# Loads, index tiles and small vector pieces of a table-building stage put at other places

## The chip, the cores and the metric

The kernel runs on one core of a Trainium2 chip. The metric is the device time of one execution in microseconds (us). The engines of the core run side by side and meet only at semaphores: TensorE (PE, with its weight loads shown as PEld), VectorE (DVE), ScalarE (ACT), GpSimd (POOL) and SyncE (SP, which issues transfers here and computes nothing). POOL issues transfers too. All transfers share 16 DMA engines.

## What is computed

One transformer layer in float32: latent cross-attention and then a gated feed-forward, each behind a layer norm and with a residual sum. The first stage, which the change touches, turns 16 context sequences of 361 rows into one table of latent and rotated keys, and folds the per-head weights.

```python
kv_c = kv @ W_kvc                       # 16 sequences, 361 rows, 512 -> 128
q_c = q @ W_dq                          # q = layernorm(x), 16 x 100 rows
k_nope = (kv_c @ W_uk); v = (kv_c @ W_uv); k_rope = _rope(kv_c @ W_kr, lk)
scores = (q_nope . k_nope + q_rope . k_rope) * scale
good = (k_ids <= qs) & (k_ids >= qs - LOOKBACK)      # qs = seg_id
scores = jnp.where(good[:, None, :, :], scores, NEG)
x = x + softmax(scores) @ v @ W_o
x = x + ffn(layernorm(x))
```

Each query looks at 9 keys only. They are gathered from the table by an index that is worked out from seg_id.

## The kernel before

Three stages follow each other: the table stage (build_setup, a block of its own that all engines enter and leave together), the attention over 5 blocks of 320 tokens, and the feed-forward over the same blocks. The change lies in the table stage.

**Turns.** The table stage has 16 turns, one for each context sequence n and, at the same time, for each head n. In each turn:
- SP loads the context `ctx_raw` (4 buffers) and the head's weights `head_w` (2 buffers). The first ones are issued ahead. From then on `head_w` n waits until turn n-2's weights have been read (`v_mm`, `r_lo`, the latter counted by DVE's last split of a turn), and `ctx_raw` n+2 follows it in the queue.
- ACT writes the high part of the context with its sums and means (`ctx_hi`, L345 to L352; 2 buffers). After that it takes the previous turn's results out of PSUM (`tab_part` L359, `wl_hi` L362, `wvo_hi` L365, `wr_hi` L368).
- DVE writes the low part (`ctx_lo`, L455) and then the previous turn's `tab` (L431) and weight remainders (L438 to L450). `tab` has 2 buffers, so L431 waits until the table store of two turns earlier has landed.
- PE multiplies the context with the folded weights: 9 high products (L487), then low and high ones (L497, L487), then the head's products with `head_w` (L509, L512). The low ones wait for `ctx_lo`. L509 waits for the load of `head_w`.
- POOL rotates the key part of `tab` (L308 to L315) and stores it into `kv_table` (L317).

Turns 0 to 3 are written out; 4 to 15 are a loop of three passes of four (`turns`).

**Small work beside the turns.** DVE's `index_work` (L404 to L419) makes the gather index `idx_all` and two mask tiles. It stands at the end of DVE's turn 0. Its seven tiles lie in the place of the second `ctx_hi` buffer, so ACT may touch that buffer only after `index_ok` (L373, at the head of its turn 1). DVE's norm pieces for the first token block (`ln.piece`: 0 to 3 statistics of a fourth of the rows, 4 the variance, 5 and 6 the normalising) stand in turns 0 (pieces 0 to 3), 1, 2 and 3. Piece 0 waits for the load of `rows` (x). POOL takes the root after its turn 0. DVE's `key_mask_work` (five operations, L395 to L399) stands behind the last turn. At the end PE turns the normalised rows (L569) and multiplies them with `wdq` (L168).

**Loads.** SP issues them in the order of its text: weights, context 0, index and mask constants, context 1, head 0, x, context 2, head 1, context 3. POOL issues five constants (`ident`, `mask`, `cosq`, `sinq`, `wdq`) before its first turn.

## Time and profile before

| | |
|---|---|
| median of 3 runs | 806.59 us (807.15, 806.59, 794.01) |
| profiled execution | 795.53 us, its span 793.9 us |
| PE busy in the span | 736.8 us (93%) |
| DVE, ACT, POOL busy | 452.4, 407.3, 196.5 us |
| table stage | 0 to 111.95 us |
| DMA over the span | 102 GB/s on average |
| loads of the table stage besides contexts and heads | weights 256 + 32 + 256 KB; index and mask 494 KB (six); x 640 KB; POOL's five constants 64 + 31.5 + 240 + 480 + 512 KB; POOL's other first ones 48 + 96 + 6 KB |

The span is the time from the first to the last instruction of the profiled execution; the device time is 1.6 us more. Where a row gives a wait, it stands in square brackets with what ended it. "x9" is a group of nine instructions that the view has merged. The three runs lie 13 us apart, and the profiled execution is near the lowest of them.

### The profile page before, as it was taken

How to read it: one execution, taken by the hardware profiler on the slowest of the kernel's cores; microseconds unless marked ns; L12 is line 12 of the kernel's file. 1: busy time of each engine (PE TensorE's matmuls, PEld its weight loads, DVE VectorE, ACT ScalarE, POOL GpSimd, SP SyncE). 2: the span in 40 equal slices, each digit the busy share in tenths (PEclk: the TensorE clock that was granted, in tenths of full speed). 3: DMA queues.
4: the chain of work that ended last, by engine and by line, in shares of the span. 5: the costliest groups of instructions: out<-in, count | busy, mean ns of one | idle time of the engine just before them, and what ended most of it. 6: DMA issues, size and time to landing. Idle time of an engine off the chain costs nothing.

```text
span 793.9 us, 18186 instructions
## 1 busy us (share of the span) xinstructions
PE 736.8 (93%) x7102; PEld 689.5 (87%) x7102; DVE 452.4 (57%) x944; ACT 407.3 (51%) x899; POOL 196.5 (25%) x330
## 2 busy tenths in 40 slices
PE   3799987789999899989999999989999999999997
PEld 3688777578997799879997899779999999999997
DVE  2887863463467555665477446755693363636342
ACT  3688834275456644575457645666577232313131
POOL 2455552542217140534044131530000000000000
PEclk9999998798999999999999999999999999999999
DMA  8899844444330533134322343047101102121021
GB/s 263 250 307 306 281 137 107 90 112 79 72 97 4 128 85 89 37 110 89 73 68 89 63 86 104 3 162 310 50 18 34 50 20 67 33 66 33 22 62 34
DMA packets 46357, 81.19 MB, mean 102 GB/s; under 512 B 5482, under 2 KB 30106, under 8 KB 46282
## 3 DMA queue, kind: packets, MB, share of 16 engines
q1 hardware_dynamic: 40796, 53.67, 26.2%
q0 software_dynamic: 5488, 26.50, 9.9%
q8 instruction: 52, 0.85, 0.5%
q14 instruction: 21, 0.17, 0.1%
HBM read 57.26 MB, written 11.28 MB: 86 GB/s over the span
## 4 chain that ended last, share of the span: by engine, by line
PE 70%; DVE 5%; ACT 4%; SPq 2%; DMA 2%; issue 1%; POOL 0%; another core or an unknown queue 0%; DVEq 0%; POOLq 0%
PE ps L1350 18%; PE ps L1059 12%; PE ps L927 9%; PE ps L1382 9%; PE ps L1064 6%; PE ps L1002 3%; PE ps L168 3%; PE ps L975 3%; SPq L827 2%; ACT q_lat L1102 2%; PE ps L937 2%; DMA key_rows<-kv_table,idx 1%; PE ps L966 1%; PE ps L991 1%; PE ps L772 1%
## 5 line engine op out<-in xcount | busy, mean ns | idle before, releaser
L1206 DVE TENSOR_TENSOR o_lo<-q_lat,o_hi 128x320 fp32r<-128x320 f32 x80 | 70.5, 887 | 81.1 <-ACT o_hi L1110 77.9
L1059 PE MATMUL ps<-o_hi,wvo_hi 128*128 128x320 f32 x320 | 96.8, 313 | 1.8 <-ACT o_hi L1110 1.8
L1110 ACT ACTIVATE o_hi<-q_lat 128x320 fp32r<-128x320 f32 x80 | 65.5, 825 | 62.2 <-PE ps L1059 61.1
L1059 PE MATMUL ps<-o_hi,wvo_lo 128*128 128x320 f32 x320 | 95.7, 310 | 0.0
L1434 ACT ACTIVATE silu<-ps,ffn_scale 128x320 f32<-128x320 f32 x55 | 29.0, 527 | 97.5 <-PE ps L1350 97.5
L869 POOL TENSOR_TENSOR rot_c<-gathered,cosq 128x192 f32<-128x192 f32 x40 | 25.4, 635 | 173.8 <-PE ps L937 143.4
L1485 DVE SCALAR_TENSOR_TENSOR hidden<-ps,ffn_scale,silu 128x320 f32<-128x320 f32 x55 | 30.2, 549 | 60.5 <-ACT silu L1434 52.8
L1059 PEld LDWEIGHTS ps<-o_hi,wvo_hi 128*128 128x128 f32 x320 | 60.6, 189 | 2.3 <-ACT o_hi L1110 2.0
L1059 PEld LDWEIGHTS ps<-o_hi,wvo_lo 128*128 128x128 f32 x320 | 60.5, 189 | 0.3
L1064 PE MATMUL ps<-o_lo,wvo_hi 128*128 128x320 f32 x320 | 60.2, 309 | 0.0
L487 PE MATMUL ps<-wkv,ctx_hi 128*128 128x384 f32 x192 | 52.9, 385 | 6.5 <-ACT ctx_hi L352 6.5
L557 POOL TENSOR_TENSOR lnf_rstd<-lnf_var,lnf_power 80x4 f32<-80x4 f32 x5 | 5.1, 1017 | 197.0 <-DVE lnf_var L551 197.0
L1350 PE MATMUL ps<-rowsT,hi_front 128*128 128x320 f32 x280 | 53.5, 308 | 0.0
L1350 PE MATMUL ps<-four,hi_front 128*128 128x320 f32 x280 | 53.1, 311 | 0.0
L1064 PEld LDWEIGHTS ps<-o_lo,wvo_hi 128*128 128x128 f32 x320 | 50.6, 189 | 0.0
L487 PEld LDWEIGHTS ps<-wkv,ctx_hi 128*128 128x128 f32 x192 | 36.4, 198 | 14.0 <-issue 13.4
L1120 ACT ACTIVATE q_lat<-ps 128x320 f32<-128x320 f32 x40 | 31.9, 798 | 32.1 <-PE ps L927 32.1
L1002 PE MATMUL ps<-probT,gathered 63*128 63x112 f32 x480 | 37.7, 290 | 11.2 <-ACT probT L1094 9.6
L1002 PEld LDWEIGHTS ps<-probT,gathered 63*128 63x128 f32 x480 | 30.6, 190 | 17.3 <-ACT probT L1094 11.8
L1350 PEld LDWEIGHTS ps<-rowsT,hi_front 128*128 128x128 f32 x280 | 44.2, 188 | 0.0
L1350 PEld LDWEIGHTS ps<-four,hi_front 128*128 128x128 f32 x280 | 43.6, 188 | 0.0
L878 POOL TENSOR_TENSOR rot<-rot_c,rot_s 128x384 f32<-128x384 f32 x40 | 42.7, 1067 | 3.1
(170 smaller groups left out, 1884.9 us busy)
## 6 DMA issues: line engine op xcount, KB each, us to landing
ctx_raw<-ctxT_dram SPq DMA_DIRECT2D x16, 722.0 KB, 7.6
gathered<-key_rows SPq DMA_DIRECT2D x240, 47.2 KB
head_w<-head_w_dram SPq DMA_DIRECT2D x16, 576.0 KB, 5.3
ffn_raw<-ffn_w_dram POOLq DMA_DIRECT2D x11, 768.0 KB, 12.8
kv_table<-tab POOLq DMA_DIRECT2D x16, 288.0 KB, 6.6
rows<-x_dram SPq DMA_DIRECT2D x5, 640.0 KB, 5.3
residual<-x_dram SPq DMA_DIRECT2D x20, 160.0 KB, 2.4
x_rows<-residual SPq DMA_DIRECT2D x20, 160.0 KB, 2.0
```

The costliest lines, as they stand in the source:

```text
L487: return pe.matmul(ps[:, b + t, 0:2 * ROW], hi[i % 2][:, c, t * P:(t + 1) * P], wkv[:, c, :], start=(c == 0), stop=(c == KC - 1), skip_gro ...
L878: pool.tensor_tensor(rot[s % 2][:, :, :, :], rc[:, :, :].unsqueeze(2).to_broadcast([GR, GROUPS, 2, R]), rs[:, :, :].unsqueeze(2).to_broadc ...
L927: last = pe.matmul(ps[:, q_bank(o), 0:TB], w[wt][:, hs, :].rearrange("p h c -> p (h c)"), xs[:, :], start=(n == 0), stop=(n == len(parts) ...
L1002: last = pe.matmul(ps[:, 6 + side, g * SK:(g + 1) * SK], kvg[keys, s, g, 0:KVC], pt[s % 2][keys, g * SK:(g + 1) * SK], start=True, stop=True)
L1059: last = pe.matmul(ps[:, 4 + m, 0:TB], w[wt][:, h, cols], o_hi[h % 2][:, :], start=(h == 0 and n == 0), stop=False, skip_group_check=True)
L1064: last = pe.matmul(ps[:, 4 + m, 0:TB], w["wvo_hi"][:, h, m * P:(m + 1) * P], o_lo[h % 2][:, :], start=False, stop=(h == H - 1), skip_group ...
L1110: act.activation(o_hi[h % 2][:, :], q_lat[:, h % 2, :, h // 2], ACT.Copy).then_inc(oh_ok, 1)
L1120: act.activation(q_dst(o), ps[:, q_bank(o), 0:TB], ACT.Copy).then_inc(q_act, 1)
L1206: dve.tensor_tensor(o_lo[h % 2][:, :], q_lat[:, h % 2, :, h // 2], o_hi[h % 2][:, :].bitcast(F32), ALU.subtract).then_inc(ol_ok, 1)
L1350: return pe.matmul(ps[:, 2 * which + c % 2, 0:TB], wt(part, c, which, k), xs[:, k, :], skip_group_check=True, **flags)
L1382: return pe.matmul(ps[:, 4 + m % 2, 0:TB], wt(part, c, 2, m), xs[:, c, :], skip_group_check=True, **flags)
L1485: dve.scalar_tensor_tensor(out=hf[:, c % 2, :], in0=ps[:, 2 + c % 2, 0:TB], scalar=scale[:, IC + c:IC + c + 1], in1=act_g[:, c % 2, :], op ...
```

## The change

It touches build_setup alone. The seven index tiles get a place of their own behind the other tiles, and ACT clears both `ctx_hi` buffers ahead of turn 0 and waits for `index_ok` no more. SP's first loads stand in another order, with x last. POOL's five constants move from ahead of turn 0 to behind its turn 2. `index_work` moves from DVE's turn 0 to its turn 1. The norm pieces 0 to 6 move to turns 4 to 10, one in each, with the root behind POOL's turn 7. The five operations of the key mask move to turns 11 to 15, one in each. DVE's and POOL's 16 turns are written out, where 12 of them were a loop.

```diff
-        with ExitStack() as index:
-            segw = sb("segw", [WROWS, BLOCKS * WSETS], I32, index)
...
+        segw = sb("segw", [WROWS, BLOCKS * WSETS], I32)
...
                 load_ctx(0, 0)
-                for dst, name in ((segw, "segw"), (segm, "segm"), (base, "row_base"), (edge_of, "edge_of")):
+                load_head(0, 0)
+                load_ctx(1, 1)
+                load_ctx(2, 2)
+                load_head(1, 1)
+                for dst, name in ((segw, "segw"), (base, "row_base"), (segm, "segm"), (edge_of, "edge_of")):
                     sp.dma_start(dst[:, :], a[name]).then_inc(seg_in, 16)
                 sp.dma_start(other32[:, :], a["other"]).then_inc(mask_in, 16)
                 sp.dma_start(blocks32[:, :], a["blocks"]).then_inc(mask_in, 16)
-                load_ctx(1, 1)
-                load_head(0, 0)
+                load_ctx(3, 3)
                 sp.dma_start(rows[:, :, :], a["x"][0:TB, :].rearrange("(t p) d -> p t d", p=LT)).then_inc(x_in, 16)
-                load_ctx(2, 2)
-                load_head(1, 1)
-                load_ctx(3, 3)
...
-                    if isinstance(n, int) and n == 0:
+                    if isinstance(n, int) and n == 2:
+                        pool.dma_start(ident[:, :], a["ident"]).then_inc(const_in, 16)
...
+                        pool.dma_start(w["wdq"][:, :, :], a["wdq"]).then_inc(const_in, 16)
+
+                for n in range(NB):
+                    rope(n, n // 4, n % 4)
+                    if n == 7:
                         ln.root(pool, 0)
-
-                turns(pool, rope)
...
-                for half in (*lo, hi[0]):
+                for half in (*lo, *hi):
...
-                    if isinstance(n, int) and n == 1:
-                        act.wait_ge(index_ok, 1)
-                        act.activation(hi[1][:, :, LK + MEANS:TROWS], zero[:, :, :], ACT.Copy)
...
-                    if isinstance(n, int) and n == 0:
+                    if n == 1:
                         index_work()
-                    if isinstance(n, int):
-                        for piece in ((0, 1, 2, 3), (4,), (5,), (6,))[n]:
-                            ln.piece(dve, 0, piece, x_in)
-
-                turns(dve, turn)
+                    elif 4 <= n < NLT + 7:
+                        ln.piece(dve, 0, n - 4, x_in)
+                    elif NLT + 7 <= n:
+                        key_mask_piece(n - NLT - 7)
+
+                for n in range(NB):
+                    turn(n, n // 4, n % 4)
                 low_weights(NB - 1, 0, NB - 1)
-                key_mask_work()
```

`key_mask_piece(k)` is operation k of `key_mask_work`, unchanged.

On SP's queue the loads ahead of the loop read as follows before the change, in the order of issue (`four` is where the folded weights' parts land, `rows` is x):

```order
L252 DMA ctx_raw<-ctxT_dram 128x4x361
L264 DMA segw<-segw_dram 126x15
L264 DMA segm<-segm_dram 128x640
L264 DMA row_base<-row_base_dram 126x15
L264 DMA edge_of<-edge_of_dram 128x2
L265 DMA other<-other_dram 128x128
L266 DMA blocks<-blocks_dram 128x189
L252 DMA ctx_raw<-ctxT_dram 128x4x361
L256 DMA head_w<-head_w_dram 128x1152
L269 DMA rows<-x_dram 80x4x512
L252 DMA ctx_raw<-ctxT_dram 128x4x361
L256 DMA head_w<-head_w_dram 128x1152
```

After the change the same queue, from the first context on:

```order
L253 DMA ctx_raw<-ctxT_dram 128x4x361
L257 DMA head_w<-head_w_dram 128x1152
L253 DMA ctx_raw<-ctxT_dram 128x4x361 x2
L257 DMA head_w<-head_w_dram 128x1152
L269 DMA segw<-segw_dram 126x15
L269 DMA row_base<-row_base_dram 126x15
L269 DMA segm<-segm_dram 128x640
L269 DMA edge_of<-edge_of_dram 128x2
L270 DMA other<-other_dram 128x128
L271 DMA blocks<-blocks_dram 128x189
L253 DMA ctx_raw<-ctxT_dram 128x4x361
L273 DMA rows<-x_dram 80x4x512
```

Head 0 and contexts 1 and 2 and head 1 have passed the index and mask constants, and x has gone behind context 3.

On DVE, from its turn 0 to the head of its turn 1, before the change (`ctx_lo` opens a turn; `lnq_st` are the norm's statistics, which wait for x):

```order
L455 TENSOR_TENSOR ctx_lo<-ctx_raw,ctx_hi 128x4x370
L405 CAST segf<-segw 126x15
L406 TENSOR_SCALAR empty<-segf 126x15
...
L416 CAST other<-other 128x128
L417 CAST blocks<-blocks 128x189
L419 MEMSET done_mark 1x1
L543 BN_STATS lnq_st<-rows 80x6 x4
L455 TENSOR_TENSOR ctx_lo<-ctx_raw,ctx_hi 128x4x370
L431 TENSOR_TENSOR tab<-ps,tab_part 128x576
```

The same engine after the change, from turn 0 to turn 2:

```order
L460 TENSOR_TENSOR ctx_lo<-ctx_raw,ctx_hi 128x4x370 x2
L436 TENSOR_TENSOR tab<-ps,tab_part 128x576
L443 TENSOR_TENSOR wl_lo<-ps,wl_hi 128x128
...
L455 TENSOR_TENSOR wr<-head_w,wr 64x64
L410 CAST segf<-segw 126x15
...
L422 CAST blocks<-blocks 128x189
L424 MEMSET done_mark 1x1
L460 TENSOR_TENSOR ctx_lo<-ctx_raw,ctx_hi 128x4x370
```

Nothing stands between the first two `ctx_lo` any more. The index operations stand behind turn 0's remainders, and the statistics are gone from here.

## Rows read from the trace of the kernel before

**Rows 1.** Chain of work that ended last, stretch 0 to 150: start, us, what.
```profile
111.95 0.02 POOLq L248
...
113.04 11.75 DMA key_rows<-kv_table,idx
```
**Rows 2.** Windows: busy us (count) of PE, PEld, DVE, ACT, POOL; clock; DMA.
```profile
9.00:26.60 17.60, 8.20 (x39) 7.01 (x39) 8.52 (x20) 9.08 (x36) 0.00 (x0) 1.00 1.04 322
26.60:30.40 3.80, 3.78 (x17) 3.78 (x18) 3.58 (x13) 0.37 (x3) 2.57 (x6) 0.55 0.18 32
35.00:96.00 61.00, 57.50 (x351) 49.99 (x350) 51.27 (x85) 50.85 (x188) 32.69 (x69) 1.00 0.96 308
14.00:16.00 2.00, 2.00 (x7) 2.00 (x8) 1.90 (x5) 0.00 (x0) 0.00 (x0) 1.00 1.07 376
```
**Rows 3.** Timeline of turns 0 and 1: start us, us, engine, line, operation, [wait].
```profile
7.84 0.84 ACT L337 ACTIVATE wkv<-four 128x768 fp32r<-128x768 f32 x1
11.12 0.51 ACT L345 ACTIVATE ctx_hi<-ctx_raw 128x361 fp32r<-128x361 f32 x1 [2.44 <-DMA ctx_raw<-ctxT_dram]
17.91 0.25 ACT L374 ACTIVATE ctx_hi<-zero 128x56 fp32r<-128x56 f32 x1 [4.20 <-DVE done_mark L419]
22.50 2.47 DVE L543 BATCH_NORM_STATS2 lnq_st<-rows 80x6 f32<-80x512 f32 x4 [4.62 <-DMA rows<-x_dram]
29.11 0.35 SPq L256 DMA_DIRECT2D head_w<-head_w_dram  x1
```
**Rows 4.** Timeline, PE: the head's products of turns 0, 2, 14 and 15.
```profile
19.31 0.71 PE L509 MATMUL ps<-head_w 128*128 128x128 f32 x4 [0.49 <-DMA head_w<-head_w_dram]
34.96 0.60 PE L509 MATMUL ps<-head_w 128*128 128x128 f32 x4
98.20 0.68 PE L509 MATMUL ps<-head_w 128*128 128x128 f32 x4 [0.72 <-DMA head_w<-head_w_dram]
103.03 0.61 PE L509 MATMUL ps<-head_w 128*128 128x128 f32 x4
```
**Rows 5.** Transfers: out, in, queue, count, KB each, median us to landing.
```profile
ctx_raw<-ctxT_dram SPq DMA_DIRECT2D x16, 722.0 KB, 7.6
head_w<-head_w_dram SPq DMA_DIRECT2D x16, 576.0 KB, 5.3
kv_table<-tab POOLq DMA_DIRECT2D x16, 288.0 KB, 6.6
wdq<-wdq_dram POOLq DMA_DIRECT2D x1, 512.0 KB, 9.0
```
**Rows 6.** Waits in 35 to 96: who, on whom: us, times, longest.
```profile
DVE tab L431 <- DMA kv_table<-tab: 4.4, 8, 1.1
DVE ctx_lo L455 <- ACT ctx_hi L352: 4.0, 7, 0.9
PE ps L509 <- DMA head_w<-head_w_dram: 3.4, 5, 1.3
```
**Rows 7.** Timeline, DVE: two `ctx_lo` without a wait between, and two pieces.
```profile
39.37 1.17 DVE L561 TENSOR_SCALAR rows<-rows,lnq_mv,lnq_rstd 80x512 f32<-80x512 f32 x2
40.46 1.69 DVE L455 TENSOR_TENSOR ctx_lo<-ctx_raw,ctx_hi 128x1480 fp32r<-128x1480 f32 x1
44.71 1.98 DVE L455 TENSOR_TENSOR ctx_lo<-ctx_raw,ctx_hi 128x1480 fp32r<-128x1480 f32 x1
```
**Rows 8.** Timeline, end of the stage: PE's product with wdq, DVE's key mask.
```profile
106.55 0.77 DVE L395 CAST key_wanted<-segm 128x640 f32<-128x640 int32 x1
107.21 4.57 PE L168 MATMUL ps<-rowsT,wdq 128*128 128x320 f32 x16 [0.53 <-ACT rowsT L578]
109.62 0.55 DVE L399 TENSOR_SCALAR edge<-key_inside,edge_of 128x640 bf16<-128x640 f32 x1
```
**Rows 9.** Timeline: one turn's tab on DVE and its store on POOL.
```profile
63.27 0.76 DVE L431 TENSOR_TENSOR tab<-ps,tab_part 128x576 f32<-128x576 f32 x1 [0.51 <-DMA kv_table<-tab]
67.23 0.80 POOL L317 DMA_DIRECT2D kv_table<-tab  x1 [0.88 <-POOL tab L315]
```

More of the change, by code:

```diff
@@ L224, in build_setup @@
         hw = [sb(f"head_w{i}", [P, HW]) for i in range(2)]
+        segw = sb("segw", [WROWS, BLOCKS * WSETS], I32)
+        base = sb("row_base", [WROWS, BLOCKS * WSETS], F32)
+        segf = sb("segf", [WROWS, BLOCKS * WSETS], F32)
+        empty = sb("empty", [WROWS, BLOCKS * WSETS], F32)
+        over = sb("over", [WROWS, BLOCKS * WSETS], F32)
+        other32 = sb("other32", [P, P], F32)
+        blocks32 = sb("blocks32", [P, GROUPS * GK], F32)
         w_in, kr_in, seg_in, rk_in, const_in, mask_in = (
@@ L237, in build_setup @@
         chain, x_in, front_in = sem("index_chain"), sem("first_rows_in"), sem("front_rows")
+        edge_ok = sem("edge_ok")
         index_ok, done_mark = sem("index_ok"), sb("done_mark", [1, 1])
@@ L294, in _ @@
                 pool.dma_start(sink[:, :, :], a["sink"]).then_inc(rk_in, 16)
-                pool.dma_start(ident[:, :], a["ident"]).then_inc(const_in, 16)
-                pool.dma_start(w["mask"][:, :], a["mask"]).then_inc(const_in, 16)
-                pool.dma_start(w["cosq"][:, :, :], a["cosq"]).then_inc(const_in, 16)
-                pool.dma_start(w["sinq"][:, :, :], a["sinq"]).then_inc(const_in, 16)
-                pool.dma_start(w["wdq"][:, :, :], a["wdq"]).then_inc(const_in, 16)
                 pool.wait_ge(rk_in, 32)
@@ L391, in link, with key_mask_piece @@
                     dve.wait_ge(chain, done[0])
-                def key_mask_work():
-                    link(dve.tensor_copy(wanted[:, :], segm[:, :]))
-                    link(dve.tensor_scalar(wanted[:, :], wanted[:, :], edge_of[:, 0:1], None, ALU.add))
-                    link(dve.tensor_scalar(inside[:, :], wanted[:, :], 0.0, float(LK - 1), ALU.max, ALU.min))
-                    link(dve.tensor_tensor(inside[:, :], inside[:, :], wanted[:, :], ALU.not_equal))
-                    link(dve.tensor_scalar(w["edge"][:, :, :].rearrange("p s x -> p (s x)"), inside[:, :],
-                                           edge_of[:, 1:2], None, ALU.mult))
+                def key_mask_piece(k):
+                    if k == 0:
+                        link(dve.tensor_copy(wanted[:, :], segm[:, :]))
+                    elif k == 1:
+                        link(dve.tensor_scalar(wanted[:, :], wanted[:, :], edge_of[:, 0:1], None, ALU.add))
+                    elif k == 2:
+                        link(dve.tensor_scalar(inside[:, :], wanted[:, :], 0.0, float(LK - 1), ALU.max, ALU.min))
+                    elif k == 3:
+                        link(dve.tensor_tensor(inside[:, :], inside[:, :], wanted[:, :], ALU.not_equal))
+                    else:
+                        dve.tensor_scalar(w["edge"][:, :, :].rearrange("p s x -> p (s x)"), inside[:, :],
+                                          edge_of[:, 1:2], None, ALU.mult).then_inc(edge_ok, 1)
                 def index_work():
```

9 lines of the change are left out of this document (3 added, 6 removed).

## The prediction

> **What bounds the kernel now.** PE is busy for 93% of the span, so I did not ask the whole span what bounds it, but the stage that is changed; nothing behind it is touched. The chain of work gives the stage's end: all engines leave the block at 111.95, and 1 us later the first gather starts, whose 11.75 us are on the chain [rows 1]. Whatever the stage loses or gains is therefore passed on in full, and the 682 us behind it are taken as unchanged.
>
> Inside the stage I asked which resource sets the pace of a turn. A turn moves 722 + 576 + 288 = 1586 KB, or 1.624 MB [rows 5]. From 35 to 96 the DMA engines have a share of 0.96 and move 308 GB/s [rows 2]. 1.624 MB at that rate are 5.27 us. PE's products with `head_w` start at 34.96 in turn 2 and at 98.20 in turn 14, so a turn takes 63.24 / 12 = 5.27 us [rows 4]. The two agree. PE alone would be quicker: from turn 14 to 15, where it waits for nothing, it takes 4.83 us [rows 4]. In that stretch it waits 3.4 us for `head_w` itself [rows 6], and it also comes later because ACT and DVE do. So from turn 2 on the stage is bound by transfers, with PE 0.44 us a turn behind.
>
> The start is different. ACT could begin context 0 when the folded weights are ready, at 7.84 + 0.84 = 8.68, but it waits for the load until 11.12. It then waits 4.20 us for DVE's index work, because of the shared place. DVE waits 4.62 us for x and only then makes turn 1's `ctx_lo`; PE waits for that in turn [rows 3]. As turn 0's remainders on DVE stand behind all this, SP can issue `head_w` 2 only at 29.11 [rows 3]. Its queue has run dry by then: from 26.6 to 30.4 the DMA engines have a share of 0.18 and move 32 GB/s [rows 2]. PE's granted clock is 0.55 of full speed in that stretch, after PE has waited.
>
> **The change part by part.**
>
> *The start.* The index tiles' own place takes ACT's 4.20 us away. The moved pieces take DVE's 4.62 us away. The loads' order takes 11.12 - 8.68 = 2.4 us off context 0, since 1327 KB of POOL's constants no longer run beside it. PE's product with `head_w` of turn 0 comes at 19.31 - 0.49 - 2.4 = 16.4. Two turns at PE's own pace later, at 16.4 + 2 x 4.83 = 26.1, comes that of turn 2, where it was at 34.96 [rows 4]. That is a lead of 8.9 us. The loads allow it: up to head 1 they are 256 + 32 + 256 + 2166 + 1152 KB and POOL's 150 KB, 4.1 MB, which at 322 GB/s [rows 2] have come some 13 us after the first start of a transfer at about 3.
>
> *What the lead is worth.* The bytes that must have come before PE's product of turn 14 are the same before and after: every context, heads 0 to 14, x, the index and mask constants and POOL's five (1327 KB, of which `wdq` is 512 [rows 5]; the others are in the table above). Only their order changes. The 1.36 MB of POOL's constants and x's 0.66 MB now fall behind turn 2, and cost (1.36 + 0.66) / 0.308 = 6.6 us there. So where transfers bound, the end moves by the DMA's idle time that is taken out, and by nothing else: 3.8 us x (1 - 32 / 308) = 3.4 us [rows 2]. The remaining 5.5 us of the lead turn into waits for `head_w` at PE. I see no new gap: x is the last of the first loads, at (4.1 + 0.5 + 0.74 + 0.66) MB / 322 GB/s + 3 = 22 us, and `head_w` 2 may be issued when turn 0's remainders are done. These ended just before 29.11, when `head_w` 2 was issued; they now start when ACT has turn 0's results, some 3 us behind 16.4, and end at about 20.
>
> *The pieces in turns 4 to 15.* DVE's turn without a wait is 44.71 - 40.46 = 4.25 us [rows 7]. The pieces are four statistics (2.47 us in all [rows 3]), the variance (0.6, an estimate: as long as one statistic), two normalisings of about 1.1 [rows 7], and the key mask, 109.62 + 0.55 - 106.55 = 3.62 [rows 8]. Together 8.9 us, or 0.74 a turn: 4.99 against the transfers' 5.27. Only the turns with a normalising, 5.35, are above it, by 0.1 us each. What covers the pieces is DVE's waiting, 4.4 + 4.0 us in the twelve turns [rows 6], most of which ends because a transfer has come. Were that cover gone, each piece would be paid. A late DVE issues `head_w` late, but there is always a context in the queue ahead of it: one lands 7.6 us after its issue, and the next head's issue comes 5 us after it [rows 5]. I take 0, with 0 and 2 us as bounds.
>
> *The index work in turn 1.* Its 2.5 us (it held ACT until 17.91 and began behind turn 0's `ctx_lo`, near 15.4) stand between turn 0's remainders (about 20) and `ctx_lo` of turn 2, needed at 24. It waits for the mask constants, which are due at about (4.1 + 0.5) / 0.322 + 3 = 17. I take 0; the bound is 1 us.
>
> *POOL.* Five issues make its rotation of turn 3 late once, by at most 5 x 0.80 = 4.0 us if each costs what the table store's issue does [rows 9], and by nothing if POOL would have waited for DVE anyway. Table stores have 2 buffers, so this reaches DVE at turn 5 and is hidden as long as transfers bound. Written out, a turn has no register work before its store; I count nothing for it.
>
> *The key mask's old place.* DVE ended there at 110.17, while PE ended at 107.21 + 4.57 = 111.78 [rows 8]. Taking it away gains nothing. PE's tail from turn 15's product to the end, 111.78 - 103.03 = 8.75 us, stays.
>
> The sum is -3.4 us against the profiled execution: 795.5 - 3.4 = 792.1, with a span of 790.5. Two of the three runs of before are near 807 and one is 13 us below, beside the profiled one, a spread four times my sum. The median of the runs is 806.6, and against it the sum gives 803.2. I state that one, since the median is the time that is compared, but the range must hold both levels.
>
> **A rule that would make more of it.** The Trainium skill, DMA: Bandwidth & Descriptors, in its Specifications, gives an HBM limit of about 358 GB/s for a core. By it a turn's 1.624 MB would be an estimated 4.54 us, under PE's 4.83, PE would set the pace, and the lead would be kept. The row for the turns does not agree with it: 308 GB/s at a share of 0.96.
>
> **The rivals.**
>
> *The lead is kept (0.18).* The engines have moved 376 GB/s where loads ran alone [rows 2]; a turn would need 1.624 / 4.83 = 336. If the 308 are no limit of the engines but what a stage in lockstep with PE, ACT and DVE asks for, PE sets the pace. Its product of turn 15 comes at 26.1 + 13 x 4.83 = 88.9 in place of 103.03: -14.1 us, 781.4 (792.5 at the median's level). Against it speaks that PE waits for `head_w` at all, and the share of 0.96.
>
> *The gap comes back elsewhere (0.12).* The two queues together run less well when POOL's constants meet the steady stream, or the index work is late. Then the end stays: 0 us, 795.5 (806.6).
>
> *The table store's loop closes (0.08), the slower side.* `tab` has 2 buffers. From DVE's `tab` to the store's issue are 67.23 - 63.27 = 3.96 us [rows 9], then 6.6 us to the landing [rows 5]: 10.6 us for two turns, the present pace. If each piece stood between a landing and the next `tab`, two of them (1.48) and a landing of 7.4 would make 12.84 us, 6.42 a turn. Then turn 15's product comes at 26.1 + 4.83 + 12 x 6.42 = 108.0, +5.0 us: 800.5 (811.6). It decides from (103.03 - 30.9) / 12 = 6.01 us a turn. For it speaks that DVE waits for this very store 8 times [rows 6]. Against it, the pieces stand ahead of `ctx_lo`, where DVE waits too. SBUF — State Buffer, section Who interferes with whom, of the Trainium skill says that a fast VectorE copy or tensor_scalar locks GpSimd out of a shared port; that would make the store later still. No row of before shows such a piece beside a store.
>
> **How the numbers follow.** The forecast (-3.4) has 0.62. Its own range is -6 to -1 us, that is 789.5 to 794.5 or 800.6 to 805.6 by the level. A measurement of this kernel can tell about 2% from no change, which is 16 us. None of the cases reaches that like for like; the largest is 14.1 us. If the levels of the two kernels should fall apart, 13 us come on top, and so I give faster 0.08, same 0.90, slower 0.02. The range takes in the forecast at both levels and no change at the upper one, 807, and half of the kept lead below the lower one, 786.
>
> **What would show it.** In the profile after: no stretch under 200 GB/s between 10 and 95 us; turn 1's `ctx_lo` near 15 and turn 2's product with `head_w` near 26; `head_w` 2 issued near 20; PE's waits for `head_w` up from 3.4 to about 8 us; turns of about 5.3 us; turn 15's product near 99.6 and the block left near 108.5. DVE's waits shrink by about the pieces' 8.9 us. The prediction is wrong if turns take 4.9 us or less (the first rival), if DVE's waits for the store grow (the third), or if something behind the stage changes its length by more than 1 us.

## The result and the profile after

| | before | after |
|---|---|---|
| median of 20 runs each, us | 796.03 (791.20 to 807.15) | 792.01 (787.27 to 805.49) |
| profiled execution, us | 795.53 | 787.27 |
| its span, us | 793.9 | 785.5 |
| its PE busy | 93% | 730.4 us, 93% |
| PE's product with `head_w` of turn 15 starts at | 103.03 [rows 4] | 97.86 |
| all engines leave the block at | 111.95 [rows 1] | 106.78 |
| from there to the end of the span | 681.95 | 678.72 |

The ratio of the times is 0.9945, with a 95% interval from 0.9927 to 0.9963: the change gains 0.55%, or 4.4 us, which is no change by the 2% that was named. The forecast of -3.4 us was nearly the size of it. The stated 803.2 is 11 us above the median of after, inside the range, and it is above before's 796.03 too. Two of before's 20 runs and five of after's lie 11 to 12 us above the others, the three runs of before that the prediction had to go by held two of these, and the ratio compares the runs without them.

The profiled execution of after is the quickest of its 20, so its own 8.3 us under the one of before (8.4 by the spans) are not the size of the change. 5.17 of the 8.4 are the stage. The other 3.23 us lie behind the stage, where no instruction was changed; 2.3 of these are one group, sixteen products of PE in the first attention block, PE's timeline of before and then of after:

```profile
182.71 6.85 PE L168 MATMUL ps<-rowsT,wdq 128*128 128x320 f32 x16
```

```profile
178.35 4.55 PE L168 MATMUL ps<-rowsT,wdq 128*128 128x320 f32 x16
```

A second profiled execution of the changed kernel (changed_again, below) took 791.96 us, 4.7 more than the first. 2.7 of these lie behind the stage as well, so the 3.23 us are little more than two executions of one program differ by.

The rows of after that answer to [rows 4], the head's products; columns as there. Shown are turns 0, 2, 5, 6, 14 and 15:

```profile
16.78 0.60 PE L515 MATMUL ps<-head_w 128*128 128x128 f32 x4
...
26.64 0.68 PE L515 MATMUL ps<-head_w 128*128 128x128 f32 x4
...
45.95 1.20 PE L515 MATMUL ps<-head_w 128*128 128x128 f32 x4 [3.21 <-DMA head_w<-head_w_dram]
52.34 0.60 PE L515 MATMUL ps<-head_w 128*128 128x128 f32 x4
...
93.05 0.68 PE L515 MATMUL ps<-head_w 128*128 128x128 f32 x4
97.86 0.61 PE L515 MATMUL ps<-head_w 128*128 128x128 f32 x4
```

Turn 2 comes at 26.64, 8.3 us ahead of before's 34.96. Between turns 2 and 6 a turn takes (52.34 - 26.64) / 4 = 6.43 us, and at turn 6 the lead is down to 3.1 us (before's turn 6 comes at 55.40). From turn 6 to 15 a turn takes (97.86 - 52.34) / 9 = 5.06, where before takes (103.03 - 55.40) / 9 = 5.29, and the lead grows again to 5.17.

Windows of after, columns as in [rows 2]. From 54 to 96 DVE, the third pair of numbers, is busy for 40.75 of 42 us:

```profile
0.00:9.00 9.00, 1.97 (x8) 1.78 (x8) 0.96 (x1) 3.45 (x9) 2.17 (x8) 1.00 0.68 209
9.00:26.00 17.00, 14.12 (x80) 12.87 (x81) 11.16 (x25) 13.26 (x51) 3.53 (x8) 1.00 1.04 321
26.00:30.00 4.00, 4.00 (x25) 3.42 (x24) 3.92 (x6) 3.14 (x13) 2.34 (x6) 1.00 0.62 193
30.00:36.00 6.00, 6.00 (x42) 5.52 (x42) 5.17 (x9) 3.91 (x15) 5.54 (x12) 1.00 0.94 299
36.00:50.00 14.00, 9.41 (x46) 7.44 (x46) 9.82 (x17) 8.37 (x33) 7.07 (x16) 0.88 1.03 388
50.00:54.00 4.00, 4.00 (x28) 3.52 (x27) 3.30 (x6) 3.33 (x14) 1.41 (x2) 1.00 0.51 137
54.00:96.00 42.00, 40.24 (x248) 35.38 (x248) 40.75 (x73) 35.60 (x131) 24.63 (x49) 1.00 0.93 302
0.00:98.00 98.00, 81.73 (x484) 71.94 (x485) 76.95 (x138) 71.07 (x259) 48.35 (x103) 0.98 0.89 293
```

And of before, for the stretches that the prediction did not look at:

```profile
0.00:9.00 9.00, 1.97 (x8) 1.78 (x8) 0.28 (x1) 3.31 (x8) 4.80 (x13) 1.00 0.67 182
9.00:26.00 17.00, 8.20 (x39) 7.01 (x39) 7.92 (x19) 8.51 (x34) 0.00 (x0) 1.00 1.05 325
26.00:34.00 8.00, 7.38 (x38) 6.90 (x39) 7.65 (x21) 4.13 (x17) 6.00 (x12) 0.79 0.50 148
30.00:32.00 2.00, 2.00 (x10) 1.52 (x10) 2.00 (x3) 1.28 (x4) 1.98 (x2) 0.92 0.92 251
32.00:34.00 2.00, 2.00 (x16) 2.00 (x15) 1.87 (x6) 2.00 (x10) 1.86 (x6) 1.00 0.79 238
0.00:103.00 103.00, 82.33 (x482) 72.26 (x483) 73.42 (x133) 71.18 (x259) 48.71 (x104) 0.98 0.88 279
```

The last row of each is the argument of the prediction in two lines. Up to turn 15's product the kernel of before moves 103 us x 279 GB/s = 28.7 MB, the changed one 98 x 293 = 28.7 MB. The bytes are the same, and what the stage gained is a higher mean rate. Where it comes from, each stretch held against the 308 GB/s of [rows 2]: before loses (308 - 148) x 8 us = 1.28 MB, or 4.2 us, in one stretch from 26 to 34. After loses (308 - 193) x 4 + (308 - 299) x 6 + (308 - 137) x 4 = 1.20 MB in three stretches, and makes up (388 - 308) x 14 = 1.12 MB between 36 and 50, which leaves 0.25 us. The first 9 us give (209 - 182) x 9 = 0.24 MB, or 0.8 us. 4.2 - 0.25 + 0.8 = 4.7 of the 5.2 us; the rest is spread over rows that differ by a few GB/s.

Of this account only the sum holds for the program. In the second execution of the changed kernel the mean up to 98 us is 293 GB/s again and turn 15 comes at 98.18, but the first 9 us have 184 GB/s, and the stretch from 50 to 54, a hole above, has none:

```profile
50.00:54.00 4.00, 4.00 (x27) 3.48 (x26) 3.47 (x6) 3.52 (x14) 2.17 (x5) 1.00 1.03 359
```

So the 0.8 us of the first 9 us are no gain of the change, and where the low stretches lie differs from one execution to the next.

SyncE's queue in after shows what stands ahead of the two low stretches at 26 and at 50; start, us, engine, line, operation:

```profile
20.85 0.58 SPq L253 DMA_DIRECT2D ctx_raw<-ctxT_dram  x1
27.28 0.34 SPq L257 DMA_DIRECT2D head_w<-head_w_dram  x1
...
43.05 0.56 SPq L253 DMA_DIRECT2D ctx_raw<-ctxT_dram  x1
51.19 0.34 SPq L257 DMA_DIRECT2D head_w<-head_w_dram  x1
```

It issues nothing for 6.4 and for 8.1 us. The issue at 27.28 waits for turn 1's remainders on DVE, which stand behind the index work. The one at 51.19 waits for turn 5's, and turn 5's product had waited 3.21 us for its `head_w`, issued at 37.25 when POOL's constants, the issues below, were in flight:

```profile
33.18 0.58 POOL L316 DMA_DIRECT2D ident<-ident_dram  x1
...
35.35 0.53 POOL L320 DMA_DIRECT2D wdq<-wdq_dram  x1
```

The waits of after between 30 and 92 us, columns as in [rows 6]:

```profile
PE ps L515 <- DMA head_w<-head_w_dram: 6.3, 4, 3.2
...
ACT ctx_hi L348 <- DMA ctx_raw<-ctxT_dram: 4.6, 2, 3.1
DVE ctx_lo L460 <- ACT ctx_hi L355: 3.9, 3, 3.0
...
DVE tab L436 <- DMA kv_table<-tab: 0.7, 1, 0.7
```

PE's waits for `head_w` are 6.3 us (4.8 in the second execution) where [rows 6] has 3.4, and DVE's waits for the table store are nearly gone, 0.7 for 4.4.

### The profile page after: what moved, and what is told of

It reads as the page before. It is cut to its first block, busy times and chain, and to the rows that moved or that the text cites. A ratio compares the mean times of both kernels' runs of the same rounds, so it can differ in the third digit from the quotient of the medians.

```text
span 785.5 us, 18041 instructions
## 1 busy us (share of the span) xinstructions
PE 730.4 (93%) x7102; PEld 684.7 (87%) x7102; DVE 455.2 (58%) x944; ACT 407.9 (52%) x899; POOL 197.0 (25%) x330
## 3 DMA queue, kind: packets, MB, share of 16 engines
q1 hardware_dynamic: 40796, 53.67, 26.1%
## 4 chain that ended last, share of the span: by engine, by line
PE 71%; ACT 4%; DVE 4%; DMA 2%; SPq 2%; issue 1%; POOL 0%; DVEq 0%; POOLq 0%
PE ps L1356 18%; PE ps L1065 12%; PE ps L933 9%; PE ps L1388 9%; PE ps L1070 6%; PE ps L1008 3%; PE ps L981 3%; PE ps L168 2%; SPq L833 2%; ACT q_lat L1108 2%; PE ps L943 2%; DMA key_rows<-kv_table,idx 2%; PE ps L972 2%; PE ps L997 1%; PE ps L778 1%
## 5 line engine op out<-in xcount | busy, mean ns | idle before, releaser
L1100 ACT ACTIVATE probT<-ps 63x336 f32<-63x336 f32 x80 | 35.3, 442 | 15.6 <-PE ps L997 11.3
```

Of the source, the lines that this page charges most:

```text
L1100: act.activation(pt[s % 2][side * HALF:side * HALF + GK, :], ps[0:GK, 4 + side, 0:GROUPS * SK], ACT.Copy).then_inc(p_ev, 1)
```

## Experiments

Two theories were held against each other from the start. By theory 1 transfers set the pace, the end moves only by the DMA's idle time that goes, and the lead is given back. By theory 2 the engines' own work and lockstep (DVE with its pieces, POOL's loop, the table store) set the pace, and what gains is moving or removing their work. Where an expectation says for its run what each theory means, that holds. "Turn 15" stands for the start of PE's head product of turn 15, "left" for the time at which all engines leave the block.

| kernel | turn 0 | turn 15 | left | us (runs) | ratio to before |
|---|---|---|---|---|---|
| before | 19.31 | 103.03 | 111.95 | | |
| pool_written_out | 19.52 | 103.08 | 112.00 | 794.62 (10) | 0.9982 [0.9955, 1.0009] |
| norm_moved | 18.74 | 98.60 | 107.52 | 791.56 (6) | 0.9939 [0.9897, 0.9982] |
| own_place | 18.77 | 102.02 | 110.95 | 793.55 (1) | |
| after | 16.78 | 97.86 | 106.78 | 792.01 (20) | 0.9945 [0.9927, 0.9963] |
| changed_again | 18.88 | 98.18 | 108.78 | 790.20 (7) | 0.9927 [0.9897, 0.9957] |
| heads_cut | 17.08 | 93.30 | 102.30 | 787.80 (1) | |
| dve_more | 17.26 | 100.69 | 109.68 | 793.35 (1) | |
| mask_last | 17.08 | 98.49 | 107.41 | 789.15 (1) | |
| consts_late | 17.40 | 95.45 | 105.64 | 791.11 (10) | 0.9940 [0.9907, 0.9973] |
| consts_first | 18.30 | 99.49 | 108.41 | 788.77 (4) | 0.9904 [0.9882, 0.9926] |
| index_last | 17.78 | 97.68 | 108.29 | 789.01 (5) | 0.9905 [0.9873, 0.9937] |
| sp_order_old | 17.42 | 97.16 | 107.77 | 801.77 (1) | |
| best | 17.21 | 95.66 | 106.27 | 789.59 (9) | 0.9924 [0.9891, 0.9957] |

The intervals of the changed kernels overlap, but for those of consts_first and after, which miss each other by 0.0001, and changed_again's overlaps both; the times rank none of them. What tells them apart is the trace of the stage, where the same kernel comes to turn 15 within 0.3 us (97.86 and 98.18). That is one pair of executions, and each other kernel has one trace, so a difference of less than about 0.5 us at turn 15 is not read as an effect. At turn 0 the same pair is 2.1 us apart (16.78 and 18.88), and no difference of that size is read as one there. The pair also shows the lead being given back: 2.1 us at turn 0 have become 0.3 at turn 15.

**pool_written_out**: the kernel before with one edit, POOL's loop written out.

```diff
-                turns(pool, rope)
+                for n in range(NB):
+                    rope(n, n // 4, n % 4)
```

> The kernel before, with POOL's 16 turns written out and nothing else changed. Theory 1 (transfers alone set the pace of a turn, 1.624 MB at 308 GB/s): the 0.4 us that POOL saves ahead of each table store are worth nothing; turn 2 to turn 14 of PE's head product stay 63.2 us apart, the stage ends at 111.9, the time is that of before within 0.5 us. Theory 2 (the table store's loop over its two buffers bounds together with the transfers): the pace falls from 5.27 towards 5.05 us a turn, DVE's waits for the store fall from 4.4 us to about 1, and the stage ends about 2 us earlier.

Measured: turn 15 at 103.08 for 103.03, and no difference in time that the interval shows. The waits between 30 and 95 us, of this kernel and then of before:

```profile
DVE ctx_lo L456 <- ACT ctx_hi L353: 7.4, 10, 1.3
```

```profile
DVE ctx_lo L455 <- ACT ctx_hi L352: 4.0, 7, 0.9
```

DVE's waits for the table store fall from 4.4 to 2.1 us, and its waits for ACT's `ctx_hi` grow from 4.0 to 7.4. The wait only changed its name. A wait that shrinks while the turns keep their length was no bound, and POOL's loop was none.

**norm_moved**: the kernel before, with only the norm's pieces moved to turns 4 to 10 (POOL's and DVE's loops written out for it, which the last run showed to be worth nothing on POOL; DVE's was not tried alone).

```diff
-                    if isinstance(n, int):
-                        for piece in ((0, 1, 2, 3), (4,), (5,), (6,))[n]:
-                            ln.piece(dve, 0, piece, x_in)
+                    if 4 <= n < NLT + 7:
+                        ln.piece(dve, 0, n - 4, x_in)
```

> The kernel before with one part of the change: the norm pieces go to turns 4 to 10, with the root behind POOL's turn 7, and DVE's and POOL's turns are written out. Loads, index work and its place as before. DVE no longer waits for x in turn 0, ACT still waits for the index work. Theory (the hole in the transfers at 26.6 to 30.4 was what DVE's wait for x cost): turn 1's ctx_lo comes at 20.7 in place of 24.9, head load 2 is issued at 25 in place of 29.1, the hole closes, and the stage ends 3 to 4 us earlier, near 108.5. If the loads' order is what matters, as x and the constants stand ahead of context 2: at most 1 us.

Measured: turn 15 comes at 98.60, 4.4 of the change's 5.2 us. Turn 1's `ctx_lo` starts at 19.98 and `head_w` 2 is issued here:

```profile
24.23 0.35 SPq L256 DMA_DIRECT2D head_w<-head_w_dram  x1
```

That is 4.9 us before the 29.11 of [rows 3]. The window where before had its hole [rows 2]:

```profile
26.60:30.40 3.80, 3.80 (x29) 3.66 (x28) 3.68 (x8) 3.74 (x16) 1.71 (x5) 1.00 0.96 348
```

348 GB/s for 32. So the norm's pieces in turns 0 to 3 are the cause of nearly all of it, and not by the time that DVE stood still: by holding the remainders of turn 0, they held SyncE's next issue, and the queue ran dry. Most of that is the wait of 4.62 us for x; the 2.47 us of statistics behind it moved with it, and no run takes the two apart. Against this kernel the whole change is only 0.4 to 0.7 us earlier at turn 15.

**own_place**: the kernel before, with only the index tiles in a place of their own and ACT's wait gone.

```diff
-                for half in (*lo, hi[0]):
+                for half in (*lo, *hi):
...
-                    if isinstance(n, int) and n == 1:
-                        act.wait_ge(index_ok, 1)
-                        act.activation(hi[1][:, :, LK + MEANS:TROWS], zero[:, :, :], ACT.Copy)
```

> The kernel before with one part of the change: the index tiles get their own place and ACT's wait for the index work goes. ACT then makes turn 1's ctx_hi up to 4 us earlier, but DVE is busy with the index work until 17.9 and waits for x until 22.5, so ctx_lo comes at 24.9 as before. Expected: 0 us, the stage ends at 112 plus or minus 0.5, head load 2 at 29.1. If ACT's wait was part of the path: up to 4 us earlier.

Measured: turn 15 at 102.02, 1.0 us earlier, of which turn 0 has 0.5. Turn 1's `ctx_lo` starts at 24.01 (24.88 in before), still behind a wait of 4.12 us for x, and `head_w` 2 is issued at 28.23. The first context was taken up 0.4 us earlier here too (10.75 for 11.12), where nothing was changed, so the 1.0 us is an upper bound. ACT's 4.20 us of [rows 3] lay beside DVE's wait for x: with one of two parallel waits gone, the other holds.

**heads_cut**: the changed kernel, but from head 2 on only the first 128 of `head_w`'s columns are loaded (its folded head weights are therefore not the model's). A turn moves less, and PE, ACT and DVE do the same work.

```diff
+                    cols = HW if isinstance(n, int) and n < 2 else P
+                    sp.dma_start(hw[i][:, 0:cols], a["head_w"][bass.ds(n, 1), :, 0:cols]
```

> The changed kernel, but from head 2 on only the first 128 of 1152 columns of the head's weights are loaded, so the folded head weights are wrong; all instructions and waits stay. That takes 512 of 1586 KB out of each turn. If transfers bound the turns: PE's waits for the head load vanish and the turns go to PE's own 4.75 to 4.83 us throughout, turn 15's head product comes near 91 in place of 97.9. If DVE with its pieces bounds now (4.25 plus 0.74 a turn): turns stay near 5.0 and turn 15's product comes near 94 or later, with DVE idle for under 0.1 us a turn.

Measured: turn 15 at 93.30, 4.6 us earlier than after. All of it is gained at the stall: from turn 2 to 6 the kernel takes 4.82 + 4.74 + 6.11 + 4.84 = 20.51 us, where after takes 25.70 and changed_again 23.25. The 6.11 is turn 5 again: its load, now of 64 KB, is issued at 36.52 and waited for until 42.62, with POOL's constants in flight beside it. From turn 6 to 15 the kernel takes 45.84, where after takes 45.52. Its turns 6 to 9 have 4.75 to 4.86 us, PE's own pace, but then turns of 5.06 to 5.47 come. DVE's timeline tells why; one turn of it, with the pieces ahead of each `ctx_lo`:

```profile
78.26 0.77 DVE L399 TENSOR_SCALAR key_wanted<-key_wanted,edge_of 128x640 f32<-128x640 f32 x1
79.06 1.70 DVE L461 TENSOR_TENSOR ctx_lo<-ctx_raw,ctx_hi 128x1480 fp32r<-128x1480 f32 x1
...
83.33 0.77 DVE L401 TENSOR_SCALAR key_inside<-key_wanted 128x640 f32<-128x640 f32 x1
84.14 1.70 DVE L461 TENSOR_TENSOR ctx_lo<-ctx_raw,ctx_hi 128x1480 fp32r<-128x1480 f32 x1
```

No row of DVE between the two `ctx_lo`, 5.08 us apart, carries a wait. So transfers bound the changed kernel up to the stall's end, and each theory is right for a part: behind it, with much of the head's bytes gone, DVE and its pieces hold the stage at the same pace that after has with all of them. The changed kernel's own rows say the same: from 54 to 96 DVE waits once, for 0.6 us, and in changed_again never, where before's DVE is busy for only 33.80 of these 42 us. That bound lies only 0.2 us a turn below the transfers' 5.27.

**dve_more**: the changed kernel with a further statistic on a tile at rest in each of turns 4 to 15, which adds DVE work and no transfer.

```diff
+                    if 4 <= n:
+                        dve.bn_stats(scratch[:, n, :], idle_in[:, :])
```

> The changed kernel with one more statistic of 512 columns on DVE in each of turns 4 to 15, of 0.62 us and 7.4 us in all; its result goes to a scratch tile that nobody reads. DVE's turn is then 4.25 + 0.74 + 0.62 = 5.6 us on average. If DVE still has cover (transfers at 5.06 to 5.27 us a turn, waits of 4.6 us left): turn 15's product comes about 12 x (5.6 - 5.27) = 4 us later, near 101 to 102, since its own pace now passes that of the transfers. If pieces cost nothing as long as any wait is left: 98 to 99. If they are paid in full: 105.

Measured: turn 15 at 100.69, 2.8 us later, for 12 x 2.47 / 4 = 7.4 us of work ([rows 3] has the length of four statistics). A wait stands in its list (30 to 92 us) that after's does not have:

```profile
PE ps L509 <- DVE ctx_lo L464: 1.9, 4, 0.8
```

So 2.8 of the 7.4 us arrive at turn 15. That is not because waits cover the rest: behind the stall there are hardly any left, and the turns grow at once. From one `ctx_lo` to the next DVE takes 0.43 to 0.61 us more than in after in turns 7 to 10, and 0.19 to 0.38 more in turns 11 to 14. The first three statistics fall ahead of the stall's end, where DVE waits anyway: at turn 6 the kernel is only 0.2 us behind after. And the key mask's pieces become shorter. The second of them, in after and then in dve_more:

```profile
82.44 0.77 DVE L398 TENSOR_SCALAR key_wanted<-key_wanted,edge_of 128x640 f32<-128x640 f32 x1
```

```profile
85.25 0.53 DVE L400 TENSOR_SCALAR key_wanted<-key_wanted,edge_of 128x640 f32<-128x640 f32 x1
```

In after it lies beside POOL's last operation on `tab`:

```profile
82.22 0.64 POOL L311 TENSOR_TENSOR tab<-rope_cos,rope_sin 128x192 f32<-128x192 f32 x1
```

In dve_more the statistic stands in front of it, and POOL is done. Four of these pieces lie ahead of turn 15's product; together they take 3.44 us in after and 2.27 in dve_more. The expected 101 to 102 was nearest, though not for the reason given, cover by transfers. That POOL's work is what lengthens the pieces is argued from the rows, no run was made for it.

**mask_last**: the changed kernel with the five key mask pieces behind the last turn, where they stood before.

```diff
-                    elif NLT + 7 <= n:
-                        key_mask_piece(n - NLT - 7)
...
+                for k in range(5):
+                    key_mask_piece(k)
```

> The changed kernel with one part undone: the five operations of the key mask stand behind DVE's last turn again. If the pieces in turns 11 to 15 are covered by transfers: turns 11 to 15 keep their pace of about 5.05 us. If DVE bounds there (with the heads cut it ran at 5.07 a turn in just these turns): they go to 4.9 us and turn 15's product comes up to 1 us earlier, near 97. DVE ends near 105 and PE's last product near 106.6, so the old place costs nothing at the end.

Measured: turn 15 at 98.49, left at 107.41, against 97.86 and 106.78 of after. DVE's waits for `ctx_hi` (30 to 95 us) are 7.1 us instead of 3.9: without the pieces DVE waits, and the turns 11 to 15 are no shorter (5.12 us on average, 5.04 in after). So DVE alone does not set their pace either; the transfers' bound of 5.27 lies right beside it, but what binds in these turns no row shows for sure. The mask pieces gained nothing and cost nothing.

**consts_late**: the changed kernel with POOL's constants later still: `ident` and `wdq` behind turn 11, mask, cosq and sinq behind turn 14.

```diff
-                    if isinstance(n, int) and n == 2:
+                    if n == 11:
...
+                    if n == 14:
+                        pool.dma_start(w["mask"][:, :], a["mask"]).then_inc(late_in, 16)
```

> The changed kernel with POOL's constants still later: ident and wdq behind turn 11, mask, cosq and sinq behind turn 14, where the engines' transfers have nearly run out; PE waits for the first two. If transfers bound up to the last head, the 752 KB that leave the bound stretch are worth 0.77 MB / 0.308 = 2.5 us, the stall of 3.2 us at turn 6 disappears, and a smaller one comes at turn 13: the stage ends 2 to 3 us before 106.7 (profile), the time is 0.3% below the changed kernel. If they were hidden anyway (their burst ran at 392 GB/s): no difference within 0.5 us.

Measured: turn 15 at 95.45, 2.4 us earlier than after. The stall at turn 5 is gone (turn 4 to 5 is one of 4.8 us) and between 36 and 50 PE is busy for 12.95 us, where it was for 9.41:

```profile
36.00:50.00 14.00, 12.95 (x80) 11.06 (x79) 12.76 (x21) 11.84 (x45) 7.68 (x16) 1.00 0.99 325
```

(The expectation counts this turn as the sixth.) It shows that it was POOL's constants that held back turn 5's `head_w`. Of the 2.4 us only 1.1 reach the end (left at 105.64): PE's last product is done at 104.20, and the block is left 1.4 us later. It is not the constants that are waited for, since SyncE's wait for `sinq` is over 2.7 us before the block is left; what remains is POOL's wait for the last table store, issued at 101.46 behind the three constants. That is argued, no run shows it. In the time nothing of it can be seen.

**consts_first**: the changed kernel with the five constants ahead of POOL's turn 0 again, as in before.

> The changed kernel with one part undone: POOL's five constants are loaded ahead of turn 0 again. Turn 0 comes 2.4 us later. Theory of bytes (the end is set by the sum of the bytes and the holes): the stall of 3.2 us at turn 6 goes, turn 15's head product stays at 97.9 plus or minus 1. If the order itself is worth something, the start's 2.4 us are lost to the end: 100.3.

Measured: turn 0 comes at 18.30 and turn 15 at 99.49, 1.3 to 1.6 us later than in the two executions of the changed kernel; the time is not worse (0.9904). The slow start is not the reason: changed_again's turn 0 is later still, and at turn 6, with no stall behind it, this kernel is ahead of both (50.97 for 52.34 and 51.98). It falls back from turn 6 to 15, at 5.39 us a turn for 5.06 and 5.13, with 4.4 us of waits for `head_w` at PE from 52 to 98 us where changed_again has 2.2. In the two others the transfers had run ahead during the stall. Why they fall behind here was not settled.

**index_last**: the changed kernel with the index work behind the last turn's low weights.

```diff
-                    if n == 1:
-                        index_work()
-                    elif 4 <= n < NLT + 7:
+                    if 4 <= n < NLT + 7:
...
+                index_work()
```

> The changed kernel with the index work behind DVE's last turn, where DVE has nothing to do while PE finishes. Head load 3 is then issued about 2.6 us earlier (27.3 to 24.7), and the hole in the transfers at 26 to 29 us (119 to 156 GB/s) closes. If transfers bound behind it, the stage ends 1 to 1.5 us earlier (the bytes that the hole did not carry). If the later stall is set by the constants alone, or the lockstep takes the lead back: 0 to 0.5 us. At the end DVE's work of 2.6 us ends before PE's last product either way.

Measured: the stretch 24 to 32 of this kernel, and then of after:

```profile
24.00:32.00 8.00, 8.00 (x54) 7.52 (x54) 6.96 (x14) 7.39 (x28) 4.85 (x11) 1.00 0.91 288
```

```profile
24.00:32.00 8.00, 7.92 (x54) 7.02 (x53) 7.75 (x15) 6.97 (x27) 4.86 (x11) 1.00 0.77 246
```

(288 - 246) x 8 us are 0.34 MB, 1.1 us at 308 GB/s; turn 15 comes at 97.68, 0.2 to 0.5 us earlier. But the hole is not closed, it lies earlier: from 20 to 24 the windows have 153 and 220 GB/s, and from 18 to 36 the mean is 266, where after has 267 and changed_again 249. Head 3 is issued at 27.10, not at the expected 24.7, since DVE waits 1.55 us for ACT where the index work stood and `ctx_lo` of turn 2 starts at 22.69 for 22.88. What the index work does is lengthen the time between the issues of heads 2 and 3: 6.98 us in both executions of the changed kernel, 5.79 here. At turn 15 that is not seen. The block is left 1.5 us later than in after, by the group in the next run.

**changed_again**: the changed kernel, a second time.

> The changed kernel once more, beside the others on the same chip: its ratio to before, expected 0.9945 plus or minus 0.002, turn 15's head product at 97.9 plus or minus 1, the stage's end between 106.5 and 108.5 depending on whether PE's clock drops before its last product.

Measured: turn 15 at 98.18, left at 108.78. Two rows of PE behind turn 15, of this execution and then of after's:

```profile
102.36 6.26 PE L168 MATMUL ps<-rowsT,wdq 128*128 128x320 f32 x16 [0.53 <-ACT rowsT L584]
```

```profile
102.04 4.57 PE L168 MATMUL ps<-rowsT,wdq 128*128 128x320 f32 x16 [0.53 <-ACT rowsT L584]
```

One and the same program takes 1.7 us longer in sixteen products. The granted clock is 0.50 from 104 to 106 in this execution and 1.00 in after's. The block left is thus a coarser measure than turn 15's product, and I read the stage by the latter.

**sp_order_old**: the changed kernel with SyncE's first loads in their order of before.

```diff
-                load_head(0, 0)
-                load_ctx(1, 1)
-                load_ctx(2, 2)
-                load_head(1, 1)
...
+                load_ctx(1, 1)
+                load_head(0, 0)
```

> The changed kernel with one part undone: SP's first loads stand in the old order, so the constants and x come ahead of context 2 and head 1. Turn 0's head weights come behind 0.49 MB more: turn 0's product at about 18.5 in place of 17, turn 1 or 2 waits for context 2 until about 20. Theory of bytes: no hole arises, turn 15's product stays within 1 us of 97.9. If the order carries gain of its own: up to 2.5 us later.

Measured: turn 15 at 97.16, turn 0 at 17.42, between the changed kernel's 16.78 and 18.88. No gain of the order of SyncE's loads is seen at either place. Behind the stage the kernel takes 800.0 - 107.77 = 692.2 us where after takes 678.7. The chain shows where most of these 13.5 us are, in the sixteen products of L168 of four blocks, of this execution and then of after's:

```profile
178.74 6.91 PE ps L168 x16
267.40 6.96 PE ps L168 x16
...
444.82 6.99 PE ps L168 x16
```

```profile
178.40 4.50 PE ps L168 x16
264.00 4.50 PE ps L168 x16
...
435.13 4.50 PE ps L168 x16
```

The four (the third are 6.97 and 4.50) differ by 9.8 us. SyncE's order can have no part in it; the last section has the clock beside it.

**best**: the changed kernel with the index work last, `ident` and `wdq` behind turn 11, and mask, cosq and sinq behind turn 13.

> The changed kernel with the index work behind DVE's last turn, ident and wdq loaded behind POOL's turn 11 and mask, cosq and sinq behind turn 13. By the two single runs: turn 15's head product came at 97.7 (index work last) and 95.5 (constants late) against 97.9. Together by the bytes that leave the bound stretch (0.77 MB / 0.308 = 2.5 us) and the hole at 26 to 29 us: 95 plus or minus 1, and the stage ends 8.9 us later, near 104, since the late constants are now issued 5 us before the last table store. That is 2.5 to 3 us below the changed kernel, 0.3 to 0.4%. If the end is held by the late constants' landing, as it was when they stood behind turn 14: 105.5.

Measured: turn 15 at 95.66, left at 106.27 with L168 at 6.26 us. The stage is 2.2 to 2.5 us shorter at turn 15 than in the changed kernel, and the time is the same: 789.59 beside changed_again's 790.20, with intervals that cover each other. Its interval against before lies below 1, and whether it beats the changed kernel can't be told.

## Why the prediction was right or wrong

- **What bounds: right for the kernel before, half of it for the changed one.** The bytes up to turn 15 are 28.7 MB in both, pool_written_out takes POOL's loop away and gains nothing, and heads_cut takes bytes away and gains 4.6 us. But it gains them up to turn 6; behind it transfers and DVE are two bounds at nearly one height (5.27 and 5.08), which the estimate of 4.99 had said and the text did not make use of. The lead that the limit of 358 GB/s in the Trainium skill (DMA: Bandwidth & Descriptors, Specifications) would have kept did not come: turns 6 to 15 took 5.06 us, not 4.83. The transfers do pass that figure here, at 388 GB/s for 14 us, but the steady turns stay under it, and DVE alone would have held them at 5.08.
- **The start: right in one execution, in part by luck.** 16.78 for 16.4, 26.64 for 26.1, turn 1's `ctx_lo` at 15.26 for 15, `head_w` 2 issued at 20.30 for 20. In the second execution these are 18.88, 28.73, 16.64 and 22.40. The term "2.4 us off context 0" was too large: ACT still waits 1.12 us for the first context in after and 1.18 in changed_again, and after's start is early because its folded weights were ready at 7.95, for 8.68 in before and 9.28 in changed_again. Which edit is worth what was not said; norm_moved and own_place show that it is the norm's pieces (4.4) far more than the tiles' place (1.0 at most). The two and the 1.3 to 1.6 us of consts_first add up to more than 5.2: they overlap, or some of them is scatter.
- **"The end moves by the DMA's idle time that is taken out": right as a rule, the term mis-sized.** 3.8 x (1 - 32 / 308) = 3.4 took the hole from 26.6 to 30.4. The rate is still low behind it (251 and 238 GB/s from 30 to 34), and counted to 34 it is 4.2 us. The 0.8 us of the first 9 us are scatter between executions: 184 GB/s in changed_again, 209 in after, 197 in norm_moved, whose first loads are those of before.
- **"I see no new gap": wrong.** Three things were missed. SyncE's issue of head 3 waits for turn 1's remainders, and the index work, costed at 0, stands ahead of them; it delays that issue by 1.2 us (index_last) and turn 15 by no more than the 1 us that was its bound. POOL's constants do not only cost bytes: they share the engines with the one load that turn 5 waits for (consts_late). And a late turn 5 makes the next issue late, which left a second hole in after and none in changed_again. It cost almost nothing in sum, because the engines ran at 388 GB/s from 36 to 50 while the constants came. Two errors cancelled, which was luck: the new holes lose 1.20 MB and the quick stretch makes up 1.12 MB. The sign "no stretch under 200 GB/s between 10 and 95 us" failed in both executions.
- **The pieces on DVE at 0: right in the number, not in the cover.** 4.99 a turn was the estimate, and 5.08 without a wait is what heads_cut shows. Behind the stall the pieces have used up DVE's waits (0.6 us in 42), and dve_more's statistics lengthen the turns at once. DVE's waits did not shrink by 8.9: those for the store fell to 0.7, while those for ACT stayed at 3.9, in one wait of 3.0 at the stall.
- **POOL written out and the key mask at 0: right** (103.08 for 103.03; 98.49 for 97.86). **POOL's issues at 0: wrong in the mechanism**, as said, by up to 2.4 us at turn 15 and by nothing that the time shows.
- **PE's waits for `head_w`, about 8: they were 6.3 and 4.8**, half of them one wait and not spread over the turns.
- **The number itself: wrong by its level.** The step that failed is "the median of the runs is 806.6, and against it the sum gives 803.2". The median of 20 runs of before is 796.03, 10.6 us below that level, and the profiled execution on which the sum was made, 795.53, lay 0.5 us from it. Against that execution the same sum gave 792.1, and that is the result I should have stated. That it meets the measured 792.0 so closely is luck: the stage gained 5.2 and 4.9 us in the two executions, where the sum had 3.4. The range has a slip as well: half of the kept lead below the lower level is 795.5 - 7.1 = 788.5 and not 786.
- **The sign "something behind the stage changes its length by more than 1 us": it did, by 3.2.** The sign could not tell anything, since two executions of the changed kernel differ by 2.7 us there.

The rival that the lead is kept fell with the stall and with DVE's bound. That the gap comes back was half true: two holes did, and were made up. The store's loop did not close: DVE's waits for it fell to 0.7 us. The prediction says that no row of before shows a piece beside a store; there are two. The normalising pieces at 33.97 and 39.37 lie beside store issues at 34.70 and 40.10, which take 0.83 and 0.81 us, where the next one, without a piece, takes 0.79. The lock that the prediction adds to this rival is not seen in the store. What is seen is the other side: a key mask piece takes 0.77 us beside POOL's work and 0.53 without it (dve_more).

## What to carry to other kernels

Follow a wait to what is queued behind it: a wait of 4.62 us on DVE, with 2.47 us of work behind it, cost the stage 4.4 because it held the instruction that frees a load's buffer, and the 4.20 us on ACT beside it cost at most 1.0. In a stretch bound by transfers, count bytes against time from the start to the last product, with the low rate behind each hole, and put late constants where no load on the path is in flight. Ask what the next bound is: here it lay 0.2 us a turn below the first. Profile the same program twice before an edit is credited with a part of a microsecond. State a forecast against the execution whose rows the sum was made of.

## What the runs showed of the hardware

The transfer rate of one stage is not one number. With POOL's constants among the loads the engines moved 388 GB/s for 14 us (389 in index_last), 348 for 3.8 us in norm_moved, and 302 to 319 in the steady turns at a share of 0.93 to 0.98. What makes the steady mix slower was not tried.

One load can be late although it is small. Turn 5's `head_w` took 8.7 us from its issue to its use with 576 KB (after) and 6.1 us with 64 KB (heads_cut), both with POOL's 1.36 MB of constants in flight; the median landing of a `head_w` of 576 KB is 5.3 us [rows 5].

VectorE's pieces are longer beside GpSimd's work. A key mask piece of 128x640 took 0.77 us where it began beside GpSimd's last operation on `tab` (after, changed_again, heads_cut), and 0.53 where that was done (dve_more), or 0.55 at the stage's end (mask_last). No run was made for this alone.

TensorE's granted clock differs between executions of one program. The sixteen products of L168 take 4.50 to 4.57 us at a granted clock of 1.00, which is 2.4 GHz, and 6.26 to 6.99 us where the clock fell to 0.50, which is 1.2 GHz. Windows around the end of block 0, of sp_order_old:

```profile
172.00:174.00 2.00, 0.34 (x2) 0.34 (x4) 1.88 (x6) 1.92 (x6) 0.00 (x0) 0.83 0.83 245
174.00:176.00 2.00, 2.00 (x25) 1.90 (x24) 0.20 (x1) 1.03 (x4) 0.00 (x0) 0.50 0.48 126
```

PE was busy for 0.34 of 2 us, in a wait of 1.68 us for `probT`, when the clock fell. In the execution of after no wait that long stands there (the longest are two of 0.78 us; PE is busy for 1.94 from 172 to 174), and the clock stays at 1.00 from 166 to 186. In before PE waits 1.16 and 0.78 us there, and the clock falls between 180 and 182. At the stage's end the same happens without a difference in the work ahead of it: PE was busy for 0.99 of the 2 us from 100 in changed_again, where the clock then fell, and for 0.80 in after, where it did not. What decides it there is open.
